# The output projection of a gated cross-attention block contracts over pairs of heads, in three passes

## The reference

```python
q = (x @ Wq).reshape(B, N, NUM_HEADS, HEAD_DIM).transpose(0, 2, 1, 3)   # B 8, N 512, 8 heads of 64
k = (context @ Wk)...                                                   # context 1024 x 256
v = (context @ Wv)...
attn = softmax(einsum('bhnd,bhmd->bhnm', q, k) * scale)
out = einsum('bhnm,bhmd->bhnd', attn, v).transpose(0, 2, 1, 3).reshape(B, N, INNER)   # INNER 512
x = x + tanh(g_xattn[0]) * (out @ Wo + bo)                              # Wo 512 x 256
x = x + tanh(g_ffn[0]) * moe(layernorm(x))                              # top 2 of 8 experts
```

## Time and profile before

| | us |
|---|---|
| median of 3 runs | 1718.18 (1717.32 to 1718.72) |
| the profiled execution, first to last instruction | 1718.5 |
| PE busy | 1647.2 (96%) |
| DVE busy | 1263.8 (74%) |
| ScalarE busy | 1049.7 (61%) |
| POOL busy | 675.1 (39%) |

### The profile page before, as it was taken

How to read it: one execution, slowest core, us unless ns; L and a number is a source line. 1 busy time by engine, 2 the same in 40 slices (tenths; PEclk the granted TensorE clock), 3 DMA queues, 4 the chain that set the end, 5 groups by cost and what they waited for, 6 DMA issues and landing times.

```text
span 1718.5 us, 33525 instructions
## 1 busy us (share of the span) xinstructions
PE 1647.2 (96%) x12454; PEld 1500.0 (87%) x12454; DVE 1263.8 (74%) x2597; ACT 1049.7 (61%) x2179; POOL 675.1 (39%) x629
## 2 busy tenths in 40 slices
PE   6999999999999999999999998979999999999997
PEld 5788888888888888888888886979999999999997
DVE  6888888888888888888888878656555556547443
ACT  5776766666766766667666766426455555546443
POOL 3352444444345345345345234313443432332322
PEclk9999999999999999999999999989999999999999
DMA  4300220121121121021031041313424421441211
GB/s 126 125 24 2 85 77 26 73 77 38 55 95 38 46 104 40 23 116 50 13 125 38 14 167 48 127 41 109 109 40 109 113 38 28 108 112 30 38 32 28
DMA packets 60555, 115.49 MB, mean 67 GB/s; under 512 B 6616, under 2 KB 48480, under 8 KB 59776
## 3 DMA queue, kind: packets, MB, share of 16 engines
q1 hardware_dynamic: 37104, 79.24, 13.0%
q0 software_dynamic: 15392, 18.66, 6.0%
q10 hardware_dynamic: 7920, 15.73, 2.7%
HBM read 90.27 MB, written 57.42 MB: 86 GB/s over the span
## 4 chain that ended last, share of the span: by engine, by line
PE 77%; DVE 12%; issue 4%; POOL 2%; ACT 2%; DMA 2%; POOLq 0%; ACTq 0%; DVEq 0%; SPq 0%
PE ring L1236 11%; PE turned L1130 11%; PE ffn L1093 10%; PE ffn L1095 10%; PE ffn L1094 10%; PE scores L1118 9%; DVE neg_max L1922 5%; PE ring L1093 4%; PE ring L1095 3%; PE ring L1094 3%; DVE pt_l L1699 3%; PE ring L1202 1%; PE ring L1204 1%; PE e_turned L1315 1%; ACT probs L1519 1%
## 5 line engine op out<-in xcount | busy, mean ns | idle before, releaser
L918 POOL TENSOR_SCALAR probs<-probs,row_rec 128x1024 f32<-128x1024 f32 x254 | 283.3, 1128 | 467.7 <-DVE row_rec L2026 456.5
L1463 ACT ACTIVATE pt_h<-turned 128x512 fp32r<-128x512 f32 x512 | 279.0, 602 | 208.3 <-PE turned L1130 208.3
L1699 DVE TENSOR_TENSOR pt_l<-turned,pt_h 128x512 fp32r<-128x512 f32 x512 | 331.7, 681 | 6.5 <-ACT pt_h L1463 6.4
L1922 DVE TENSOR_REDUCE neg_max<-scores 128x1 f32<-128x1024 f32 x256 | 302.3, 1217 | 35.1 <-PE scores L1118 35.0
L1130 PE MATMUL turned<-ident,probs 128*128 128x128 f32 x2048 | 281.9, 279 | 27.2 <-DVE pt_l L1699 19.6
L1130 PEld LDWEIGHTS turned<-ident,probs 128*128 128x128 f32 x2048 | 224.5, 141 | 95.2 <-issue 61.8
L1519 ACT ACTIVATE probs<-scores,neg_max 128x1024 f32<-128x1024 f32 x256 | 285.6, 1117 | 13.9 <-DVE neg_max L1922 12.7
L1236 PE MATMUL ring<-pt_h,v_hl 128*128 128x256 f32 x1024 | 262.7, 294 | 0.9
L1236 PE MATMUL ring<-pt_l,v_hl 128*128 128x256 f32 x1024 | 252.2, 284 | 0.0
L1236 PEld LDWEIGHTS ring<-pt_h,v_hl 128*128 128x128 f32 x1024 | 196.8, 192 | 5.0 <-issue 3.6
L2292 DVE TENSOR_TENSOR act_f<-ffn,silu 128x256 f32<-128x256 f32 (+1 forms) x232 | 108.5, 468 | 122.4 <-ACT silu L1633 115.9
(11 more groups left out here) (260 smaller groups left out, 3911.0 us busy)
## 6 DMA issues: line engine op xcount, KB each, us to landing
lists<-pads SPq DMA_DIRECT2D x8, 4160.0 KB
w_raw<-w_t ACTq DMA_DIRECT2D x10, 1024.0 KB, 8.6
e_rows<-lists SPq DMA_DIRECT2D x26, 390.0 KB
ctx_raw<-ctx_t SPq DMA_DIRECT2D x15, 512.0 KB, 3.7
wg_raw<-wg_t ACTq DMA_DIRECT2D x5, 1024.0 KB, 7.9
x_in<-x SPq DMA_DIRECT2D x8, 512.0 KB, 3.9
x_sum<-x SPq DMA_DIRECT2D x8, 512.0 KB, 3.9
out<-x_sum SPq DMA_DIRECT2D x8, 512.0 KB, 3.0
```

Source lines behind the costliest of these rows:

```text
L918: nc.gpsimd.tensor_scalar(probs[:, k, :], probs[:, k, :], row_rec[:, k:k + 1], 1.0, ALU.mult, ALU.mult).then_inc(scaled, 1)
L1463: return nc.scalar.activation(dst, src, ACT.Copy)
L1699: return nc.vector.tensor_tensor(dst, src, hi_part.bitcast(F32), ALU.subtract)
L1922: nc.vector.tensor_reduce(neg_max[:, k:k + 1], scores[:, n % 2, :].rearrange("p (a c) -> p a c", a=2), AX.XY, ALU.max, negate=True).then_i ...
```

## The change

The o job's stationary block now holds, for the first head of a pair, high then low parts and for the second head low then high. The high products of the two heads thus land on rows 0 to 63 and 64 to 127, the two halves of one pair. The drain writes three tiles of a pair: `ot_h` (high part of the high product, ScalarE), `o_low` (the low product, ScalarE) and `o_rest` (what `ot_h` leaves of the high product, DVE). POOL adds `o_rest` and `o_low` to `ot_l`, one addition of 128x256 for every two o jobs (`join_low`), in the steps with u % 4 equal to 3, ahead of all but the scaling. A w job takes, for each of two pairs, three passes over 128 rows: 6 matmuls in place of 8. PE waits for the join by a new semaphore `ot_done`. Wo is loaded once, in one transfer, and split by one copy and one subtraction. In `FIRST_JOBS` three w jobs stand one step later. Behind the last batch the last join stands between the first five and the last five of the ten weight subtractions.

```diff
-    15: [("w", 0, 0)],
-    16: [("w", 0, 1), ("k", 3, 0)],
-    17: [("v", 1, 3)],
+    16: [("w", 0, 0), ("k", 3, 0)],
+    17: [("v", 1, 3), ("w", 0, 1)],
...
-    19: [("w", 0, 2), ("l", 0, 0)],
-    20: [("k", 3, 1), ("q", 3, 0)],
+    19: [("l", 0, 0)],
+    20: [("w", 0, 2), ("k", 3, 1), ("q", 3, 0)],
...
+LOWS_AHEAD = 5
...
-        wo_h = tile(attn, "wo_h", [P, H, D], F32R)
-        wo_x = tile(attn, "wo_x", [P, H, D], F32R)
+        wo_h = tile(attn, "wo_h", [P, PAIRS, D], F32R)
+        wo_l = tile(attn, "wo_l", [P, PAIRS, D], F32R)
+        o_rest = tile(attn, "o_rest", [P, 2, N])
+        o_low = tile(attn, "o_low", [P, 2, N])
...
-        ot_h = tile(attn, "ot_h", [P, H // 2, N], F32R)
+        ot_h = tile(attn, "ot_h", [P, 2, N], F32R)
+        ot_l = tile(attn, "ot_l", [P, 2, N], F32R)
...
-        v_hl = tile(attn, "v_hl", [P, KT, H, P], F32R)
+        v_hl = tile(attn, "v_hl", [P, 2, KT, 2, 4, DH], F32R)
...
             def load_wo():
-                for half in range(2):
-
-                    if half == 0:
-                        sp.wait_ge(weights_split, 3)
-                    else:
-                        sp.wait_ge(first_pads, 16)
-                    for copy_ in range(2):
-                        sp.dma_start(wo_raw(half)[copy_ * DH:(copy_ + 1) * DH, :, :],
...
+                sp.wait_ge(weights_split, 3)
+                sp.dma_start(x_sum[:, :, :], wo.rearrange("(g p) d -> p g d", p=P))\
+                    .then_inc(raw_loaded[3], 16)
...
+            def join_low(body, u):
+
+                i = ((u - 6) // 4 * 2 + 1) % (2 * H)
+                part, m = i // 4 % 2, i // 2 % 2
+                toks = slice(m * 2 * P, (m + 1) * 2 * P)
+                wait_drained(pool, body, body.where[("o", i, 0)])
+                nc.gpsimd.tensor_tensor(ot_l[:, part, toks], o_rest[:, part, toks], o_low[:, part, toks],
+                                        ALU.add).then_inc(ot_done, 1)
...
+                    if u % 4 == 3 and body is not END and (body.prev if u < 4 else body.own):
+                        join_low(body, u - 1)
...
                         pool.wait_ge(listed, 16 * 2 * QT * (B - 1))
-                        for p in FIRST_LOWS:
+                        for p in FIRST_LOWS[:LOWS_AHEAD]:
+                            low_first(p)
+                        join_low(body, 2)
+                        for p in FIRST_LOWS[LOWS_AHEAD:]:
                             low_first(p)
...
-                    o = ("o", H * i + H // 2 + 1 + j // 2 * 2, 0)
-                    reads = [body.before.where[o] - RING if i == 1 and j < 2 else body.where[o]]
+                    pe.wait_ge(ot_done, at(b - 1 if i == 1 else b, H, 4 * i + 3 + j // 2))
...
                     toks = slice(j * P, (j + 1) * P)
-                    for h in range(H // 2):
-                        head = i * (H // 2) + h
-                        nc.tensor.matmul(bank[:, 0:D], ot_h[:, h, toks], wo_h[:, head, :],
-                                         start=h == 0, stop=False)
-                        last = nc.tensor.matmul(bank[:, 0:D], ot_x[:, h, toks], wo_x[:, head, :],
-                                                start=False, stop=h == H // 2 - 1)
+                    for part in range(2):
+                        pair = 2 * i + part
+                        last = passes(bank[:, 0:D], (ot_h[:, part, toks], ot_l[:, part, toks]),
+                                      (wo_h[:, pair, :], wo_l[:, pair, :]), part == 0, part == 1)
...
                 if kind == "o":
-                    h, ab = i // 4 * 2 + i % 2, i % 2
+                    pair, ab = i // 4, i % 2
                     for kt in range(KT):
+                        values = v_hl[:, pair // 2, kt, pair % 2, 2 * ab:2 * ab + 2, :]\
+                            .rearrange("p s d -> p (s d)")
                         for part in (pt_h, pt_l):
-                            last = nc.tensor.matmul(bank[:, 0:2 * P], v_hl[:, kt, h, :],
-                                                    part[:, ab, kt, :],
+                            last = nc.tensor.matmul(bank[:, 0:2 * P], values, part[:, ab, kt, :],
...
-                    hi(ot_x[0:DH, h % 4, toks], bank[0:DH, 0:2 * P])
-                    last = hi(ot_h[:, h % 4, toks], bank[:, 0:2 * P])
+                    main, low = slice(ab * DH, (ab + 1) * DH), slice((1 - ab) * DH, (2 - ab) * DH)
+                    hi(ot_h[main, pair % 2, toks], bank[main, 0:2 * P])
+                    last = hi(o_low[main, pair % 2, toks], bank[low, 0:2 * P])
...
-                    if body is FIRST and u in (5, 6):
-                        half = u - 5
-                        part = slice(half * 4, half * 4 + 4)
-                        act.wait_ge(raw_loaded[3 + half], 16 * 2)
-                        hi(wo_x[DH:P, part, :], wo_raw(half)[DH:P, :, :])
-                        hi(wo_h[:, part, :], wo_raw(half)).then_inc(raw_hi, 1)
+                    if body is FIRST and u == 5:
+                        act.wait_ge(raw_loaded[3], 16)
+                        hi(wo_h[:, :, :], x_sum[:, :, :]).then_inc(raw_hi, 1)
...
-                    last = lo(ot_x[DH:P, h % 4, toks], bank[0:DH, 0:2 * P], ot_h[0:DH, h % 4, toks])
+                    main = slice(ab * DH, (ab + 1) * DH)
+                    last = lo(o_rest[main, pair % 2, toks], bank[main, 0:2 * P], ot_h[main, pair % 2, toks])
...
-                    if body is FIRST and u in (7, 8):
-                        half = u - 7
-                        part = slice(half * 4, half * 4 + 4)
-                        split_raw(3 + half, wo_raw(half)[0:DH, :, :], wo_x[0:DH, part, :],
-                                  wo_h[0:DH, part, :])
+                    if body is FIRST and u == 7:
+                        split_raw(3, x_sum[:, :, :], wo_l[:, :, :], wo_h[:, :, :])
```

More of the change, by code:

```diff
@@ L291, in build @@
         pt_l = tile(attn, "pt_l", [P, 2, KT, 2 * P], F32R)
-        ot_x = tile(attn, "ot_x", [P, H // 2, N], F32R)
+        tile(attn, "spare", [P, 4, N])
         neg_max = tile(attn, "neg_max", [P, 4])
@@ L386, in build @@
         small_loaded = sem("small_loaded")
-        raw_loaded = [sem(f"raw_loaded{i}") for i in range(5)]
+        raw_loaded = [sem(f"raw_loaded{i}") for i in range(4)]
         consts = sem("consts")
@@ L405, in build @@
         filled = sem("filled")
+        ot_done = sem("ot_done")
         drained = [sem("drained0"), sem("drained1")]
@@ L496, in whole @@
             return t[:, :, :].rearrange("p c n -> p (c n)")
-        def wo_raw(half):
-            return x_sum[:, :, :] if half == 0 else rows[:, :, 0:D]
         def first_ctx_raw(half):
@@ L633, in load_wo @@
             def load_wo():
-                for half in range(2):
-                    if half == 0:
-                        sp.wait_ge(weights_split, 3)
-                    else:
-                        sp.wait_ge(first_pads, 16)
-                    for copy_ in range(2):
-                        sp.dma_start(wo_raw(half)[copy_ * DH:(copy_ + 1) * DH, :, :],
-                                     wo[half * (INNER // 2):(half + 1) * (INNER // 2), :]
-                                     .rearrange("(h p) d -> p h d", p=DH))\
-                            .then_inc(raw_loaded[3 + half], 16)
+                sp.wait_ge(weights_split, 3)
+                sp.dma_start(x_sum[:, :, :], wo.rearrange("(g p) d -> p g d", p=P))\
+                    .then_inc(raw_loaded[3], 16)
                 sp.wait_ge(weights_split, 4)
@@ L1147, in wait_for_job @@
                     if body is FIRST and j == 0:
-                        pe.wait_ge(weights_split, 5)
-                    o = ("o", H * i + H // 2 + 1 + j // 2 * 2, 0)
-                    reads = [body.before.where[o] - RING if i == 1 and j < 2 else body.where[o]]
+                        pe.wait_ge(weights_split, 4)
+                    pe.wait_ge(ot_done, at(b - 1 if i == 1 else b, H, 4 * i + 3 + j // 2))
                 if kind == "x":
@@ L1494, in drain @@
                 if kind == "v":
-                    last = hi(v_hl[:, 2 * j:2 * j + 2, 4 * i:4 * i + 4, 0:DH],
-                              bank.rearrange("p (t h d) -> p t h d", t=2, d=DH))
+                    part = v_hl[:, i, 2 * j:2 * j + 2, :, :, :].rearrange("p t g s d -> p (t g) s d")
+                    last = hi(part[:, :, 0:4:3, :], bank.rearrange("p (g a d) -> p g a d", a=2, d=DH))
                 if kind == "o":
-                    h, m = i // 4 * 2 + i % 2, i // 2 % 2
+                    pair, m, ab = i // 4, i // 2 % 2, i % 2
                     toks = slice(m * 2 * P, (m + 1) * 2 * P)
-                    hi(ot_x[0:DH, h % 4, toks], bank[0:DH, 0:2 * P])
-                    last = hi(ot_h[:, h % 4, toks], bank[:, 0:2 * P])
+                    main, low = slice(ab * DH, (ab + 1) * DH), slice((1 - ab) * DH, (2 - ab) * DH)
+                    hi(ot_h[main, pair % 2, toks], bank[main, 0:2 * P])
+                    last = hi(o_low[main, pair % 2, toks], bank[low, 0:2 * P])
```

(11 more changed lines are left out.)

## The result

Four runs of the changed kernel have a median of 1729.46 us (1727.97 to 1730.28), four of the kernel before beside them 1718.45 us (1717.32 to 1719.13). The ratio is 1.0069, 95% interval 1.0057 to 1.0080: 0.7% slower. Forecast were 1720.7 us and a range up to 1727, so the time lies 2.5 us outside. The profiled execution took a span of 1728.6 us.

The account below looks back on a forecast made before the run. PE is busy 96% but has short waits for DVE and POOL. Terms -3.6 + 8.3 - 4.9 + 2.6 = +2.4 us on 1718.5 us (0.3 above the runs' median) gave 1720.7 us, range 1711.5 to 1727.

Parts of the forecast that it names:

- I cost it at nothing: Draining an o job: still two ScalarE copies and one DVE subtraction of 256 columns, only partitions differ; cost nothing.
- The first batch's w jobs move one step later, past no wait but their own join: First batch's job table: the later w jobs were said to meet no other wait; no cost was counted.
- with one exception, step 11: POOL's join ahead of normalise delays the scaling PE waits for, 1.2 us in each of seven batches: 8.3 us loss.
- The w jobs, -3.6: Output projection with fewer matmuls: 15 jobs keep their 0.24 us saving, the others only lengthen PE's waits; 3.6 us gained.
- Loading Wo, -4.9: First batch: removed ScalarE copies and DVE subtraction shorten PE's wait and keep its clock up; 4.9 us gained.
- The end, +2.6: Behind the last batch: a join among POOL's ten weight subtractions makes them end 2.6 us later; 2.6 us loss.
- The first 1.3: Last batch, step 31: the last join delays the scaling and the turn behind it by 1.3 us, contained in 2.6.
- the third rival: Clock at the last scaling: PE's longer wait drops its clock to 0.50, costing 2.5 us, 1723.2 us; chance 0.13.
- The shared port: 64 POOL joins each hold a small two-input DVE operation by 0.1 us: 6 us, 1727 us; chance 0.12.

Follow-up runs that it names:

- experiment 1: Changed kernel with the join at the end of step 11 moved behind step 12's two scalings in each batch; 1721.33 us, 1.0024 times the kernel before.
- e5_w6: Kernel before with the last head of each half left out of the output projection, 6 matmuls per w job; 1796.28 us, 1.0467, with later routing changed.
- e10_onecopy: Changed kernel without POOL's joins and without ScalarE's copy of the low product, which is left out of the sum; 1709.06 us, 0.9954.
- e4_before_rows: Kernel before with the first of ScalarE's two o-bank copies reading rows 64 to 127 instead of 0 to 63; 1720.54 us, 1.0024.
- e14_same: Changed kernel without joins, low product left out, ScalarE's second copy reading the same bank rows as the first; 1715.37 us, 0.9982.
- e2_q30: Changed kernel with the first batch's Q projection of pair 3 moved from step 20 to step 15; 1727.04 us, 1.0047.
- e15_vector_table: Changed kernel with VectorE adding the low product, no joins, and the kernel before's first-batch table (w jobs at steps 15, 16, 19); 1723.03 us, 1.0028.
- e9_nojoin: Changed kernel without POOL's joins, the low product left out of the sum, ScalarE still making both copies; 1718.18 us, 1.0005.
- e8_extra: Changed kernel with the removed first-batch work on the output weights put back (ScalarE's second copies, VectorE's second subtraction); 1731.54 us, 1.0087.
- e7_all: Changed kernel with step 11's join behind step 12's scalings, pair 3's Q projection at step 15, and POOL's last-batch order changed; 1718.89 us, 1.0013.

## Why the prediction was wrong

**"I cost it at nothing" (draining an o job) is the step that failed first.** The term measured about 5 us in seven batches and up to 1.65 in the first, most of the 8.8 us between forecast and time. It compared widths and missed that the kernel before's two copies begin at the same row and overlap. ScalarE's exp behind them stands on PE's chain at steps 2, 10, 14 and 24. In the account these are +0.10, +0.15, +0.21 (what experiment 1 leaves of step 14) and +0.26: 0.7 us a batch. At step 2 what the shorter w job gives (0.13 in e5_w6) is already taken off; by e10_onecopy the second copy costs 0.9 a batch. That the second copy is late for its start rows is shown by e4_before_rows and e14_same, that those steps hang on it by e10_onecopy. The changed kernel's two copies read different rows, and the overlap is gone.

**"The first batch's w jobs move one step later, past no wait but their own join"** failed next. At step 20 three jobs share two banks, and the third waits for VectorE: 1.5 us (e2_q30, e15_vector_table).

**Joins, "with one exception, step 11".** The mechanism was right and the size too large: 0.85 us a batch and 5.9 in all for 1.2 and 8.3. PE's stall did grow by 1.08 (0.45 to 1.53), but a part of step 14's delay would have been there for ScalarE's sake (0.22 by e10_onecopy). A middle batch took 132.6 us where 132.2 were forecast. And it was not the only exception: step 27 of the last batch has scatters between join and scaling, +1.32 at step 30, which e9_nojoin gives back, and the join of step 7 costs the first batch 0.2.

**The w jobs, -3.6.** Right, in places and in size: e5_w6 gives 0.63 us per middle batch where 0.48 was counted, the changed kernel shows 0.47 at the two places.

**Loading Wo, -4.9.** It measured -4.83 between the two traces, but 3.3 to 3.8 is the removed work (3.3 were worked out for it); the rest is a fall of the granted clock that one execution had the earlier trace rows. The prediction took it for what follows such a wait, though PE waited as long (1.94 us) in e4_before_rows and e8_extra, and so counted some 1.5 us that the timed runs need not have.

**The end, +2.6.** +0.65 behind step 30. The first 1.3 came as 1.1 (2.73 us of wait for 1.63 in the earlier trace rows), and then the clock fell (mean 0.67 from 1084 to 1088 us), as the third rival said: the next turn took 1.94 us for 1.16, though the end as a whole lost less than that rival's 2.5. The last subtraction on POOL ended at 1101.43 us, 3.7 us later than before when counted from step 30's scores, where 2.6 were worked out; PE hardly felt it. The joins there cost 1.8 us by e9_nojoin, with what the clock fell behind them.

**The shared port** did not show: e9_nojoin takes all 64 joins away, and every step but those behind them in POOL's queue keeps its time to 0.02 us in the median of the middle batches.

Put together (the forecast of 1720.7 is 1720.6 by its own terms): 2.4 as forecast, -2.4 (step 11's size), +5 and +1.6 (ScalarE), +1.5 (table), +1.3 (step 27), +0.2 (step 7), -2.0 (the end), +1.5 (the clock near 62 us): 9.1 us, against 9.7 by the account; both rise by 0.8 if the timed runs of the kernel before have the short fall near step 30, which no run settles. The medians say 11.0, and the stretch behind the last r job varies by more than what is missing: the last one or two microseconds stay open.

## What to carry to other kernels

An edit that changes only where an operand begins is not free: look in the timeline whether the instruction overlaps its predecessor now, and whether it still will. Work moved off the busiest engine is paid on whichever chain it lands; here the low product cost 9 us on ScalarE and 9 more in POOL's queue, or 16 to 17 on VectorE alone, while 128 matmuls gave 4. Before putting a short operation into an in-order queue, find the place where that queue waits for something else anyway: between the two closing scalings PE did not wait for the join, in front of them it did. And a clock level seen once behind a wait is a fact of one execution until a second trace shows it.

## What the runs showed of the hardware

In the o jobs of these traces ScalarE started a second copy, or the exp behind the copies, before the previous copy had ended only where both begin at the same rows. The second copy of an o job started 0.28 us behind the first with equal rows (before, e14_same) and 0.39 with others (changed kernel, e4_before_rows), in the median of the 128 jobs of each trace. Other rows of the input are enough (e4_before_rows, where both outputs begin at row 0), and so are other rows of the output: in the changed kernel the second head's o_low reads from row 0 as the exp does, but writes from row 64, and the exp starts 0.40 behind it. The Trainium skill, VectorE: DVE Perf Modes, section Two Vector instructions with no wait between them, says the like of VectorE: an instruction is held back until the earlier ones have finished when its input or output starts in another quadrant (group of 32 partitions) than the last one's in the same memory. The traces here show the like on ScalarE, for rows 0 and 64.

The granted clock does not repeat from one execution to the next even where PE's waits do. Behind the wait of 1.9 us near 60 us it was 0.50 from 62 to 64 us in the kernel before and 1.00 in e4_before_rows and e8_extra. Behind the waits of 2.61 and 1.07 us of the last batch it was low for about 7 us in the kernel before and e9_nojoin and for 3 in e4_before_rows and e7_all, and the step took 11.7 us in the first two and 10.9 in the others.
